# The D term of a Mamba-2 block moved from TensorE to ScalarE and VectorE

## The reference, cut to what matters

```python
# per chunk c, 128 rows; 4 heads of 64 columns, D_INNER = 256, D_STATE = 64
xBC = silu(conv(x @ W_in))               # xh | B | C
dt  = softplus(dt + dt_bias);  dA = dt * A;  A_cum = cumsum(dA)
Y_diag = (C B^T * L) @ (xh * dt)         # inside the chunk
Y_off  = (C @ prev_state) * exp(A_cum)   # from the state before it
Y = Y_diag + Y_off + xh * D[:, None]     # D: one number per head
Y = Y * silu(z);  Y = Y * rsqrt(mean(Y*Y) + EPS) * norm_w
out = (Y @ W_out) @ W_lin + b_lin
```

## Time and profile before

| what | value |
|---|---|
| median of 3 runs | 876.24 us (873.51 to 878.65) |
| profiled execution | 873.88 us, span 872.2 us |
| mean granted TensorE clock | 0.969 of full speed |
| busy: PE, DVE, ACT, POOL | 803.9, 775.1, 673.5, 573.7 us |

### The profile page before, as it was taken

The page is one execution under the profiler, slowest core; times in us unless marked ns, Lnnn a source line. Parts: engine busy times, 40 slices in busy tenths (PEclk is TensorE's granted clock), DMA queues, the critical chain, the costliest instruction groups (busy, mean ns, idle before and its releaser), DMA issues. The chain is left out here.

```text
span 872.2 us, 22186 instructions
## 1 busy us (share of the span) xinstructions
PE 803.9 (92%) x6654; PEld 764.2 (88%) x6654; DVE 775.1 (89%) x1965; ACT 673.5 (77%) x1402; POOL 573.7 (66%) x1141
## 2 busy tenths in 40 slices
PE   3978999998998999995989999999999999999965
PEld 1667999998998999985989999999999999999954
DVE  6557899997999899978699999999999999999952
ACT  6566888876878878885588888788888888888761
POOL 4462366655666566678678778777787777877841
PEclk9798999999999999998999999999999999999987
DMA  6456969786878778602212112111111121110000
GB/s 196 126 166 179 313 220 305 240 279 221 258 263 263 260 226 284 222 33 63 71 48 64 62 41 67 47 54 61 41 63 60 39 66 39 60 38 19 5 6 11
DMA packets 97547, 110.74 MB, mean 127 GB/s; under 512 B 6464, under 2 KB 89280, under 8 KB 97472
## 3 DMA queue, kind: packets, MB, share of 16 engines
q1 hardware_dynamic: 97472, 109.74, 39.6%
HBM read 90.85 MB, written 18.87 MB: 126 GB/s over the span
## 5 line engine op out<-in xcount | busy, mean ns | idle before, releaser
L1094 ACT ACTIVATE maskA<-code 128x1024 fp32r<-128x1024 int8 x256 | 268.3, 1050 | 47.4 <-DVE code L683 26.6
L1346 PE MATMUL accA<-Y,maskA 128*128 128x260 f32 (+1 forms) x1792 | 273.2, 296 | 13.2 <-issue 7.5
L1356 PE MATMUL accC<-Y,maskC 128*128 128x260 f32 (+1 forms) x1792 | 256.1, 286 | 3.2 <-DVE maskC L691 3.2
L691 DVE TENSOR_SCALAR maskC<-code 128x1024 fp32r<-128x1024 int8 x256 | 252.8, 988 | 0.2
L1346 PEld LDWEIGHTS accA<-Y,maskA 128*128 128x128 f32 x1792 | 235.1, 193 | 16.8 <-issue 9.9
L1356 PEld LDWEIGHTS accC<-Y,maskC 128*128 128x128 f32 x1792 | 232.5, 192 | 4.0 <-DVE maskC L691 4.0
L683 DVE SCALAR_TENSOR_TENSOR code<-f_rows,neg_f,ps 128x512 int8<-128x512 f32 x256 | 178.4, 739 | 37.7 <-PE ps L1286 36.1
L1034 ACT ACTIVATE edges<-adj_in 128x1024 bf16<-128x1024 f32 x128 | 133.1, 1044 | 22.8 <-DMA adj_in<-in_adj_dram 15.1
L1286 PE MATMUL ps<-ident,edges 128*128 128x128 bf16 x1024 | 81.6, 223 | 12.1 <-ACT edges L1034 7.8
L928 DVE SCALAR_TENSOR_TENSOR room<-room 128x128 f32<-128x128 f32 x288 | 92.0, 341 | 0.0
L1286 PEld LDWEIGHTS ps<-ident,edges 128*128 128x128 bf16 x1024 | 59.6, 99 | 23.0 <-DVE code L683 7.2
(11 more groups left out here) (229 smaller groups left out, 1611.0 us busy)
## 6 DMA issues: line engine op xcount, KB each, us to landing
adj_in<-in_adj_dram SPq DMA_DIRECT2D x128, 512.0 KB, 4.6
edge_codes<-code SPq DMA_DIRECT2D x8, 2048.0 KB, 10.0
code<-edge_codes SPq DMA_DIRECT2D x32, 512.0 KB, 3.3
xn<-in_x_dram SPq DMA_DIRECT2D x4, 512.0 KB, 5.4
room<-in_x_dram SPq DMA_DIRECT2D x32, 64.0 KB, 1.8
room<-in_L_gnn_h_dram SPq DMA_DIRECT2D x32, 64.0 KB, 1.9
out_dram<-room SPq DMA_DIRECT2D x32, 64.0 KB, 1.6
room<-in_L_ffn_W_in_dram SPq DMA_DIRECT2D x1, 192.0 KB, 2.6
```

Source lines behind the costliest of these rows:

```text
L691: v.tensor_scalar(maskC[:, b % MASKS], src, 2.0, None, ALU.is_equal).then_inc(S["maskC_ready"], 1)
L1094: s.activation(maskA[:, b % MASKS], src, ACT.Relu, bias=-2.0).then_inc(S["maskA_ready"], 1)
L1346: t_.matmul(accA[k][:, 0:2 * cols], maskA[:, b % MASKS, l * P:(l + 1) * P], y2_of(jt, 0) if cols == F else Y[:, jt, 0, :, 0:cols], start=j ...
L1356: m = t_.matmul(accC[k][:, 0:2 * cols], maskC[:, b % MASKS, l * P:(l + 1) * P], y2_of(jt, 1) if cols == F else Y[:, jt, 1, :, 0:cols], sta ...
```

## The change

D's term leaves TensorE. `skip_w`, the two diagonal matrices, and the matmuls with them are gone, and each of the four `wmix` matmuls starts its own sum. ScalarE, which already reads the turned x from PSUM for `xdt`, reads it four more times, times D of the head, into a new buffer `xskip` in SBUF, between B's copy and `xdtd`. VectorE's one multiply in `y_state` becomes four instructions, one per head, that multiply and add `xskip`. D is loaded as a row of four numbers on all partitions (one transfer) and not as a column (two transfers).

```diff
@@ SP
-            for dst, src, n in ((b_row, b_lin, P), (dt_b, dt_bias, NH), (a_row, A_log, NH)):
+            for dst, src, n in ((b_row, b_lin, P), (dt_b, dt_bias, NH), (a_row, A_log, NH), (d_row, D, NH)):
                 sp.dma_start(dst, src.rearrange("(o c) -> o c", o=1).broadcast_to([P, n])).then_inc(S["w_in"], 16)
-            heads_of = D.rearrange("(k h) -> h k", h=P // HD)
-            for h in range(P // HD):
-                sp.dma_start(d_col[h * HD:(h + 1) * HD], heads_of[h:h + 1].broadcast_to([HD, KB]),
-                             allow_slow_non_contiguous=True).then_inc(S["w_in"], 16)
@@ DVE, weights()
-                for kb in range(KB):
-                    v.tensor_scalar(skip_w[:, kb], ident[:], d_col[:, kb:kb + 1], None, ALU.mult).then_inc(S["skip_ready"], 1)
@@ DVE, y_state()
                         dve.wait_ge(S["ps_ready"], s_ - 3)
-                        summed_y[0] = step(v.tensor_tensor(heads(ysum), heads(ps[0][:, DI:2 * DI]),
-                                                           tiny[:, 4 + k2, 0:NH].unsqueeze(2).broadcast_to([P, NH, HD]), ALU.mult))
+                        dve.wait_ge(S["skip_ready"], s_ - 3)
+                        for h in range(NH):
+                            mine = slice(h * HD, (h + 1) * HD)
+                            summed_y[0] = step(v.scalar_tensor_tensor(out=ysum[:, mine], in0=ps[0][:, DI + h * HD:DI + (h + 1) * HD],
+                                                                      scalar=tiny[:, 4 + k2, h:h + 1], in1=xskip[:, k2, mine],
+                                                                      op0=ALU.mult, op1=ALU.add))
@@ ACT, slot()
                     s.copy(bl, ps[2][:, P + DI:P + DI + P]).then_inc(S["bl_ready"], 1)
+                    for h in range(NH):
+                        last = s.activation(xskip[:, kc, h * HD:(h + 1) * HD], ps[2][:, P + h * HD:P + (h + 1) * HD], ACT.Copy,
+                                            scale=d_row[:, h:h + 1])
+                    last.then_inc(S["skip_ready"], 1)
@@ PE, slot()
                         pe.wait_ge(S["bl_ready"], s_ - 3)
+                        pe.wait_ge(S["skip_ready"], s_ - 3)
@@ PE, the chunk's output group
-                    if isinstance(s_, int) and s_ == 4:
-                        pe.wait_ge(S["skip_ready"], KB)
-                    for kb in range(KB):
-                        t_.matmul(ps[0][:, kb * P:(kb + 1) * P], xbc[:, (k - 4) % 2, kb, :], skip_w[:, kb], start=True, stop=False)
-                        for h in range(kb * P // HD, (kb + 1) * P // HD):
-                            t_.matmul(ps[0][:, h * HD:(h + 1) * HD], wmix[:, h], xdt[:, h * HD:(h + 1) * HD], start=False,
-                                      stop=h == (kb + 1) * P // HD - 1)
+                    for h in range(NH):
+                        t_.matmul(ps[0][:, h * HD:(h + 1) * HD], wmix[:, h], xdt[:, h * HD:(h + 1) * HD], start=True, stop=True)
```

More of the change, by code:

```diff
@@ L181, in gnn_ffn_kernel @@
         a_row = rows_space.take(NH)
-        d_col = rows_space.take(KB)
+        d_row = rows_space.take(NH)
         upto = rows_space.take(P)
@@ L209, in gnn_ffn_kernel @@
         xdtd = rows_space.take(DI)
-        skip_w = adj_space.take(KB, P)
+        xskip = adj_space.take(2, DI)
         yg = rows_space.take(DI)
@@ L609, in slot @@
                 end_chain()
-            pool.wait_ge(S["w_in"], 16 * 13)
+            pool.wait_ge(S["w_in"], 16 * 12)
             schedule(g, slot)
@@ L838, in weights @@
             def weights():
-                dve.wait_ge(S["w_in"], 16 * 13)
+                dve.wait_ge(S["w_in"], 16 * 12)
                 v.tensor_scalar(w_zdt[:, 0:DI], w_zdt[:, 0:DI], 0.5, None, ALU.mult)
@@ L1267, in slot @@
                 if isinstance(s_, int) and s_ == 0:
-                    act.wait_ge(S["w_in"], 16 * 13)
+                    act.wait_ge(S["w_in"], 16 * 12)
                     s.activation(a_row, a_row, ACT.Exp).then_inc(S["w_ready"], 1)
@@ L1397, in turn_weights @@
             def turn_weights():
-                pe.wait_ge(S["w_in"], 16 * 13)
+                pe.wait_ge(S["w_in"], 16 * 12)
                 for kb in range(KB):
```

## The result

The kernel after takes 887.81 us (882.33 to 889.90, 4 runs) against 875.52 us (873.51 to 878.65, 4 runs) on the same chips: a ratio of 1.0117, interval 1.0069 to 1.0164. Run once more beside other kernels it gave 1.0116 (1.0089 to 1.0143). By the ratio that is 10.2 us more (the two medians lie 12.3 us apart), where 4.8 us were forecast. Its profiled execution took 882.33 us, 8.4 us over that of before.

The account below looks back on a forecast made before the run. The prediction took VectorE with GpSimd as the bound, TensorE close behind. 4.5 us in the slots plus 0.3 in the drain made 4.8, taking the median from 876.24 to 881.0 us; range 869 to 891.

Parts of the forecast that it names:

- the forecast's own path: Whole kernel: VectorE's added work less one absorbed wait; 877 to 885 us, chance 0.45.
- the signs of being wrong: Profile after: a 12.9 us slot, VectorE idle until ScalarE's L1221 ends, or L1010 over 2 us long.
- The bound: Full slots: VectorE with GpSimd sets the 13.465 us slot; TensorE waits, so its 0.61 us saved counts nothing.
- VectorE's queue: Full slot before: VectorE's queue has no hole; two masks stand still behind GpSimd, for 1.71 and 0.26 us.
- VectorE's price: y_state: four instructions at 0.195 us cost 0.78; less L947's 0.34, 0.44 us of added work a slot.
- The absorbed wait: Mask behind L1000: its vanished stall pays 0.28 of 0.44 us, leaving 0.16 a slot, 4.5 us over 28 slots.
- The port: VectorE and GpSimd's shared port: L589 still waits for L1010, and the mask beside L589 stays at about 2.4 us.
- rival 5: Shared port: GpSimd's L587 or L589 gets in first, L1010 stalls, not the mask; 870 to 882 us, chance 0.10.
- ScalarE, "I add nothing": ScalarE's chain to the convolution: 0.79 us added against 0.87 of slack, so nothing counted.
- The drain: Slots 32 to 35: TensorE gives back 2.3 us, ScalarE adds 2.4, VectorE some 0.2; together +0.3 us.

Follow-up runs that it names:

- pe_alone: Kernel before without the L1467 matmuls, D's term left out and nothing in its place; 877.93 us, ratio 0.9997.
- before_mask_free: Kernel before with one of VectorE's four masks in a form that also adds up its result, moved ahead of L1010; 871.91 us, ratio 0.9924.
- dve_alone: Kernel before with VectorE's part only: y_state's multiply becomes four multiply-adds that add a buffer of zeros; 884.97 us, ratio 1.0087.
- dve_eight: Kernel before with VectorE's part only, in eight instructions of 32 columns and not four of 64; 896.61 us, ratio 1.0227.
- after_mask_free: Kernel after with one of VectorE's four masks in a form that also adds up its result, moved ahead of L1008; 881.73 us, ratio 1.0044 to before.
- act_alone: Kernel before with ScalarE's four added activations and their wait only, into a buffer nobody reads; 884.36 us, ratio 1.0077.

## Why the prediction was right, and where its size was off

The time lies in the stated range of 869 to 891 us and moved the way that was forecast. It lies outside the 877 to 885 us that the forecast's own path was given, and the change is over twice its 4.8 us. The full slots came out near the forecast although the stall changed its place, which was one of the signs of being wrong; the miss came from ramp and drain, and the wide range covered it. That is luck and not foresight.

- **The bound.** Right. TensorE's 0.61 us a slot were worth nothing (`pe_alone`), and to free VectorE from GpSimd was worth 0.28 us (`before_mask_free`).
- **VectorE's queue.** "No hole" was read a little too well: 3.3 us of idle time stand ahead of L901 in 21 slots, 0.16 a slot, behind VectorE's own L896. And besides the two masks that were named the one at 708.22 stood still, too. Neither changes the sum.
- **VectorE's price.** Right: 0.19 us a step and 0.77 in all, where 0.195 and 0.78 were taken from L908 and the slope of L1006 to L1010. By the Trainium skill (VectorE: DVE Perf Modes, the section on the TRN2 errata) a step is (120 + 64) / 0.96 = 192 ns, an estimate with which the trace agrees (0.19 us apart). For one instruction of 256 columns the same formula gives 0.39 us, and there the trace differs: L947 held the queue for 0.34. So the work added is 0.77 - 0.34 = 0.43 us, and not the 0.375 worked out from the page.
- **The absorbed wait.** Right: the mask behind L1000 paid with 0.25 us, and the full slots took 3.8 us where 4.5 were forecast; the unrolled ones grew by 0.10 us and not by 0.16 (13.36 to 13.46). About the first 0.24 us of VectorE's added work were free (0.43 added, 0.19 counted in `dve_alone`) and the next were not (`dve_eight`).
- **The port.** This part of the mechanism was wrong, and rival 5, with a chance of 0.10, happened: L587 and L589 got in ahead, L1010 stands still and not the mask. As rival 5 said, the sum is nearly the same in the full slots; its 870 to 882 us were missed through ramp and drain.
- **ScalarE, "I add nothing".** In the full slots this holds, but for another reason than mine. Alone its delay costs 0.15 us a slot, at L885 and not at the convolution; in the change VectorE is late by as much, so the two don't add (13.66 and 13.61 alone, 13.62 together). In the ramp it doesn't hold, and I never looked there. TensorE's wait for L1202 in slot 3, in the waits view before and then after:

```profile
PEld ps L1454 <- ACT room L1202: 1.9, 1, 1.9
PE ps L1454 <- ACT room L1202: 1.7, 1, 1.7
```

```profile
PEld ps L1457 <- ACT room L1200: 2.8, 1, 2.8
PE ps L1457 <- ACT room L1200: 2.6, 1, 2.6
```

ScalarE's added 0.8 us go straight into it, and behind that longer idle time of TensorE the clock is granted at 1.2 and not 2.4 GHz for 3.4 us (0.94 over the ramp, 1.00 before). Every profile with ScalarE's work in it has that window near slot 4, but for `after_mask_free`; none without it has. The wait goes with it: TensorE's longest there is 2.5 to 2.6 us in the six profiles with the window and at most 1.7 in the seven without, `after_mask_free` among them. +1.3 us.
- **The drain.** This is the step that was mis-sized: +0.3 forecast, +4.4 measured. The last two passes of the chain can be laid side by side, from the start of L1518 (849.22; L1516 after, 855.76) to the span's end. They take 23.0 us before and 24.8 after. Chain that ended last, before and then after:

```profile
856.26 0.57 PE ps L1490 x2
860.27 0.73 PE ps L1518 x4
867.52 0.45 PE ps L1502 x2
```

```profile
862.61 1.06 PE ps L1488 x2
875.72 0.70 PE ps L1500 x2
```

In these two passes:

- ScalarE's steps add 0.8 us. From the start of its four `xdt` steps (L1249, L1247 after) to that of L1518 it is 2.40 us before and 3.18 after, in each of the last three passes of the drain, as forecast.
- VectorE's add 0.5, where 0.2 were forecast.
- TensorE gives back 1.5 and not 2.3: L1468's eight records take 1.97 us on their own, where those of L1469 took 1.50 between those of L1467.
- The forecast had nothing for the clock. The mean granted clock is 0.50 here in the kernel after and 0.72 before, and steps of TensorE that are the same in both take 2.1 us more: L1518's second time 0.73 and 1.24, L1477 to L1492 1.8 and 3.2, L1502 0.45 and 0.70. Without that the two passes would have been some 0.3 us shorter than before, an estimate from these rows.

The other 2.5 us lie in the drain's first 30 us. ScalarE's work takes 2.1 of them, in two passes at 0.8 us and 0.5 in the one ahead of them, which the forecast didn't count; 0.4 us are not divided, at a clock of 0.78 against 0.88. In `dve_alone`, too, only 0.4 of the 2.5 us are VectorE's own steps in the last two passes, and 1.7 are TensorE's at half clock.

Whether the change brings the lower clock isn't shown, as no kernel held it fixed and all but the kernel after were profiled once. Over the whole drain it is 0.81 in the kernel before and in `before_mask_free`, 0.71 and 0.70 in the two that only lack L1467, 0.75 and 0.76 in `act_alone` and `dve_alone`, and 0.66 in both profiles of the kernel after.

## What to carry to other kernels

A busy share of 99% says nothing until a known instruction is compared with itself: the same mask took 0.69, 0.95, 1.10 and 2.40 us, and the largest excess was part of the bound. Before work is moved off a full engine, take it away altogether once and look at the slot: here that gave 0.9997 and would have ended the idea. And follow a delay to every instruction that waits for what is queued behind it, in the ramp and the drain as well as in the full slots: more than half of the loss lay in those two.

## What the runs showed of the hardware

- The masks' form that also adds up its result took 1.21 us for 128 x 1024 beside a GpSimd multiply with two inputs in SBUF, with no stall; the plain form took 0.68 alone and 2.40 behind it.
- Who stands still can turn on some tenths of a microsecond. L589, started 0.21 us after L1010 (704.45 and 704.24), waited for it; L585, started 0.12 us ahead of L1008, did not, and L1008 stood still for 1.7 us. In one kernel, `dve_alone`, both happened.
- TensorE's same instructions took 0.73 and 0.45 us at the full granted clock and 1.24 and 0.70 at half (L1518, L1502).
- A four-column instruction with two inputs in SBUF is held up like a wide one: 0.37 us in place of 0.15.
